# Attention kernel on one core: the last transpose of each turn group reads plain float32, and the mask matmul moves one place forward

## The chip, the core and the metric

The kernel runs on one core of a Trainium2 chip. The metric is the device time of one launch in microseconds (us); the median of three runs is compared. The core has a matrix engine (PE, with its weight loads shown apart as PEld), a vector engine (DVE), an activation engine (ACT), a general engine (POOL), and a queue engine (SP) that issues most of the transfers. Each engine works through its own list in order and waits for semaphores that the others raise.

## The reference

For 4 sequences of 1024 tokens of width 256, with 16 heads of head width 128 plus 64 rotary columns:

```
xn     = layernorm(x)
kv_c   = xn @ W_kvd + b_kvd;   q_c = xn @ W_qd + b_qd            # 64 and 192 wide
keys   = [heads(kv_c @ W_ku + b_ku), rope(heads(kv_c @ W_kr + b_kr))]
query  = [heads(q_c @ W_qu + b_qu),  rope(heads(q_c @ W_qr + b_qr))]
scores = query . keys / sqrt(192), causal
ctx    = softmax(scores) @ heads(kv_c @ W_vu + b_vu)
out    = x + ctx @ W_o + b_o + xn @ binarized(W_ffn).T + b_ffn
```

## The kernel before, in words

The weight products are folded once at the start, so that a head's keys and values are the 64-wide latent itself. Precision is kept by splitting operands into a high and a low part, each in the 4-byte single-pass format (float32r), and adding the products.

The heads go in pairs: 8 pairs for each of 4 sequences, so 32 pair steps. A pair step has 4 blocks, g, numbered n = 0 to 3 inside the pair. A block takes one long and one short row tile of 128 queries, (7,0), (6,1), (5,2), (4,3), for both heads, which makes 4 score items (g, x) with x from 0 to 3, and 9 tiles of 128 keys for each head. The scores of an item go into one of two PSUM slots, `ring[0]` and `ring[1]`, which items and the projections of the next pair use in turn. DVE takes them out with their row minimum (`minimum`, L1086, semaphore `min_ready`); ACT makes the exponentials (L788, `exp_ready`), which lie in `probs` as float32; `probs_r` is the same memory under the single-pass type.

The exponentials must be transposed before they are multiplied with the values. That is done in 5 turn groups for each block, 640 in all: 4 of them have 2 key tiles, so 4 transposes of 128x128, and one has a single tile, so 2 transposes. `turn_group` writes a group into one of two PSUM banks `turn` and raises `turn_full` with its last transpose. ACT copies the bank to `probs_hi` (L797), DVE subtracts to make `probs_lo` (L1096) and raises `turned_ready`, after which the bank is free for the group after the next, and `weigh_group` (L1585, L1586) may multiply. ACT then takes the product out (`u_hi`, L802), PE multiplies with the output weights (`output`, L1609, L1610) and DVE accumulates (L1133).

The causal mask is a bfloat16 matmul of an identity with a mask tile (`mask`, L1522): it opens the accumulation in the score slot of a later item, and the score matmuls (L1539 to L1541) add to it. It is issued inside a turn group, ahead of that group's last transpose. Before it, PE waits until the slot has been left (`slot_left`): by `minimum` of the item two entries earlier, or by ACT's copy (L702) of a projection (L1509). There are 512 masks.

All orders, on PE as on ACT and DVE, are written out by hand: each engine has a `sequence(g)` with the steps of the four blocks. On PE a pair step is, in short: projection of the next pair's rotary keys, output, two turn groups, weighing, scores, and so on, with 20 turn groups, 15 of which carry masks. In three of the 8 pair steps of a sequence, the first three sequences also do the next sequence's work: float32 transposes of its normalized input (`begin("transpose")`, L1437, written with the same call as the turn groups but with plain float32 operands), its down projections (L1448), its feed-forward product (L1454) and its natural-order latent (L1464).

Of the kernel before, what the change touches and what calls it, by code (L numbers as in the profile page):

```python
# [34 lines left out]
P = 128  # L35
# [62 lines left out]
def is_block(g):  # L98
    return 0 <= g < STEPS * BLOCKS
# [36 lines left out]
def build(nc, x, W_kvd, b_kvd, W_ku, b_ku, W_vu, b_vu, W_kr, b_kr, W_qd, b_qd, W_qu, b_qu, W_qr, b_qr,  # L136
# [21 lines left out]
    with ExitStack() as ctx:  # L158
        def sb(name, shape, dt=F32):
            return ctx.enter_context(nc.sbuf_tensor(name, shape, dt))  # L160
# [4 lines left out]
        ident_r, ident_bf, mask_bf = sb("ident", [P, P], F32R), sb("ident_bf", [P, P], BF16), sb("mask_bf", [P, P], BF16)  # L165
        ident = ident_r[:, :].bitcast(F32)
# [65 lines left out]
        turn = [ctx.enter_context(nc.psum_tensor(f"turn{i}", [P, 512], F32)) for i in range(2)]  # L232
        turn_r = [bank[:, :].bitcast(F32R) for bank in turn]
# [61 lines left out]
        def slot_of(entry):  # L295

            return ITEM[entry] % 2
# [9 lines left out]
        def groups_of(g):  # L307

            return [(w, qt, kt, min(2, qt + 1 - kt)) for w, qt in enumerate(LONG_SHORT[g % BLOCKS])
                    for kt in range(0, qt + 1, 2)]  # L310

        def probs_of(g, w, h):

            long, short = LONG_SHORT[g % BLOCKS]
            return probs[g % 2][h][:, (long + 1) * P * w:][:, 0:((long, short)[w] + 1) * P]

        def probs_turned(g, w, h, kt):

            long, short = LONG_SHORT[g % BLOCKS]
            return probs_r[g % 2][h][:, ((long + 1) * w + kt) * P:][:, 0:P]  # L320
# [1080 lines left out]
        def _(pe):  # L1401
            def slot_left(entry):


                if ITEM[entry] < 2:
                    return
                what, owner, k = ENTRIES[ITEM[entry] - 2]
                if what == "score":
                    pe.wait_ge(min_ready, owner * SCORE_ITEMS + k + 1)
                elif what == "project":  # L1410
                    pe.wait_ge(evacuated, owner * PROJ_ITEMS + k + 1)
                elif what == "transpose":
                    pe.wait_ge(xnt_ready, owner * 2 + k + 1)
                elif what == "down":
                    pe.wait_ge(down_ready, owner * 2 + k + 1)
                elif what == "linear":
                    pe.wait_ge(linear_ready, owner * 2 + k + 1)
                elif what == "bias":
                    pe.wait_ge(bias_left, 1)
                else:  # L1420
                    pe.wait_ge(nat_left, owner * 2 + k + 1)
# [94 lines left out]
            def mask(g, x):  # L1516

                if not is_block(g):
                    return
                qt, entry = LONG_SHORT[g % BLOCKS][x % 2], ("score", g, x)  # L1520
                slot_left(entry)
                pe.matmul(ring[slot_of(entry)][:, KEY_COLUMN[qt] + qt * P:KEY_COLUMN[qt] + (qt + 1) * P], ident_bf[:, :], mask_bf[:, :],  # L1522
                          start=True, stop=False, skip_group_check=True)
# [21 lines left out]
            def turn_group(g, i, *masked):  # L1545

                if not is_block(g):
                    for block_g, x in masked:
                        mask(block_g, x)
                    return  # L1550
                w, qt, first_kt, tiles = groups_of(g)[i]
                r = g * GROUPS + i
                if first_kt == 0:
                    pe.wait_ge(exp_ready, g * SCORE_ITEMS + 3 + w)
                if r >= 2:

                    pe.wait_ge(turned_ready, r - 1)
                for t in range(tiles):
                    for h in range(2):
                        kt = first_kt + t  # L1560
                        if (t, h) == (tiles - 1, 1):
                            for block_g, x in masked:
                                mask(block_g, x)
                        mm = pe.transpose(turn_r[r % 2][:, (2 * t + h) * P:(2 * t + h + 1) * P],  # L1564
                                          probs_turned(g, w, h, kt), ident_r[:, :])
                mm.then_inc(turn_full, 1)

            def weigh_group(g, i):
# [56 lines left out]
            def sequence(g):  # L1625
# [3 lines left out]
                if n == 0:  # L1629
                    project(g, ROPE_K)  # L1630
                    output(g - 3, 1)
                    turn_group(g - 1, 0)
                    turn_group(g - 1, 1, (g, 0))
                    weigh_group(g - 2, 3)
                    weigh_group(g - 2, 4)
                    head_ready(g, 0)
                    scores(g, 0, 0)
                    scores(g, 0, 1)
                    turn_group(g - 1, 2, (g, 1))
                    output(g - 2, 0)  # L1640
                    weigh_group(g - 1, 0)
# [244 lines left out]
```

## Time and profile before

| | |
|---|---|
| median of 3 runs | 1408.62 us (1408.5 to 1410.0) |
| the profiled execution's own time | 1410.69 us |
| its span in the profile | 1408.9 us |
| mean granted clock of TensorE | 0.997 of full speed |
| busy: PE, PEld, DVE, ACT, POOL | 97%, 87%, 81%, 85%, 71% |

The span is the time from the first to the last instruction of the profiled execution. PE's busy time is the union of its matmul records; one record lasts from its start to a modelled end, and records of neighbours overlap. The distance from one start to the next is therefore more telling than the length of a record.

### The profile page before, as it was taken

How to read it: one execution, taken by the hardware profiler on the slowest of the kernel's cores; microseconds unless marked ns; L12 is line 12 of the kernel's file. 1: busy time of each engine (PE TensorE's matmuls, PEld its weight loads, DVE VectorE, ACT ScalarE, POOL GpSimd, SP SyncE). 2: the span in 40 equal slices, each digit the busy share in tenths (PEclk: the TensorE clock that was granted, in tenths of full speed). 3: DMA queues.
4: the chain of work that ended last, by engine and by line, in shares of the span. 5: the costliest groups of instructions: out<-in, count | busy, mean ns of one | idle time of the engine just before them, and what ended most of it. 6: DMA issues, size and time to landing. Idle time of an engine off the chain costs nothing.

```text
span 1408.9 us, 27603 instructions
## 1 busy us (share of the span) xinstructions
PE 1373.1 (97%) x9786; PEld 1229.7 (87%) x9786; DVE 1146.4 (81%) x2708; ACT 1200.5 (85%) x2603; POOL 1000.4 (71%) x573
## 2 busy tenths in 40 slices
PE   6979999999999999999999999999999999999998
PEld 4769999997898999888899999999789999999987
DVE  4858898885788888887688889888678888888898
ACT  4659889997788988998788999899878988889887
POOL 6986777777667777769666787777766877777750
PEclk9999999999999999999999999999999999999999
DMA  9851222212343322211333222222233322221110
GB/s 274 228 127 50 72 54 64 64 50 64 76 107 79 83 64 64 64 34 47 79 94 92 64 80 64 65 57 57 63 77 87 88 64 65 64 60 45 40 31 31
DMA packets 46957, 106.82 MB, mean 76 GB/s; under 512 B 9333, under 2 KB 17830, under 8 KB 46822
## 3 DMA queue, kind: packets, MB, share of 16 engines
q1 hardware_dynamic: 43360, 94.01, 26.0%
q0 software_dynamic: 3296, 11.01, 2.8%
q8 instruction: 80, 1.31, 0.4%
q14 instruction: 55, 0.45, 0.1%
q10 hardware_dynamic: 166, 0.03, 0.0%
HBM read 48.92 MB, written 9.96 MB: 42 GB/s over the span
## 4 chain that ended last, share of the span: by engine, by line
PE 79%; ACT 7%; POOL 5%; DVE 5%; DMA 2%; issue 1%; SPq 1%; POOLq 0%; ACTq 0%; DVEq 0%
PE ring L1509 11%; PE turn L1564 10%; PE u_ps L1585 9%; PE ring L1539 9%; PE ring L1540 8%; PE ring L1541 8%; PE u_ps L1586 8%; PE o_ps L1609 4%; PE o_ps L1610 4%; PE ring L1522 3%; ACT probs L788 2%; PE ring L1448 2%; PE ring L1454 2%; DVE probs L1086 1%; DVE probs_lo L1096 1%; POOL k_rope L377 1%
## 5 line engine op out<-in xcount | busy, mean ns | idle before, releaser
L1086 DVE TENSOR_SCALAR_CACHE_REDUCE probs<-ring,c_t 128x1024 f32<-128x1024 f32 (+7 forms) x512 | 413.2, 809 | 85.7 <-PE ring L1541 85.2
L1096 DVE TENSOR_TENSOR probs_lo<-turn,probs_hi 128x512 fp32r<-128x512 f32 (+1 forms) x640 | 401.0, 630 | 65.7 <-ACT probs_hi L797 61.0
L797 ACT ACTIVATE probs_hi<-turn 128x512 fp32r<-128x512 f32 (+1 forms) x640 | 346.4, 550 | 94.0 <-PE turn L1564 91.2
L788 ACT ACTIVATE probs<-probs,row_min 128x1024 f32<-128x1024 f32 (+7 forms) x512 | 394.5, 772 | 11.8 <-DVE probs L1086 9.5
L1564 PE MATMUL turn<-ident,probs_r 128*128 128x128 f32 x2304 | 315.9, 244 | 4.6 <-DVE probs_lo L1096 2.7
L1585 PE MATMUL u_ps<-probs_hi,kv_nat 128*128 128x256 f32 x1147 | 313.5, 301 | 1.2 <-DVE u_pair L1102 1.2
L1564 PEld LDWEIGHTS turn<-ident,probs_r 128*128 128x128 f32 x2304 | 267.9, 141 | 36.5 <-DVE probs_lo L1096 15.3
L1586 PE MATMUL u_ps<-probs_lo,kv_nat 128*128 128x256 f32 x1147 | 289.7, 281 | 0.0
L1539 PE MATMUL ring<-k_hi,q_hi 128*128 128x512 f32 (+3 forms) x768 | 273.6, 356 | 0.0
L1540 PE MATMUL ring<-k_lo,q_hi 128*128 128x512 f32 (+3 forms) x768 | 262.9, 342 | 0.0
L1541 PE MATMUL ring<-k_hi,q_lo 128*128 128x512 f32 (+3 forms) x768 | 262.7, 342 | 0.0
L1133 DVE SCALAR_TENSOR_TENSOR acc<-o_ps,row_inv,acc 128x256 f32<-128x256 f32 x474 | 227.0, 479 | 31.6 <-PE o_ps L1610 28.2
L1585 PEld LDWEIGHTS u_ps<-probs_hi,kv_nat 128*128 128x128 f32 x1147 | 216.2, 189 | 5.4 <-DVE u_pair L1102 1.8
L1586 PEld LDWEIGHTS u_ps<-probs_lo,kv_nat 128*128 128x128 f32 x1147 | 217.1, 189 | 0.0
L388 POOL TENSOR_TENSOR k_lo<-k_rope,k_hi 64x1024 fp32r<-64x1024 f32 x62 | 148.5, 2396 | 48.7 <-ACT k_hi L766 46.3
L377 POOL TENSOR_TENSOR q_x<-q_x,cos 64x1024 f32<-64x1024 f32 x31 | 74.5, 2404 | 129.3 <-DMA swapped<-q_x 129.3
L377 POOL TENSOR_TENSOR k_rope<-k_rope,cos 128x1024 f32<-128x1024 f32 x31 | 74.6, 2407 | 128.2 <-DMA swapped<-k_rope 127.9
L1541 PEld LDWEIGHTS ring<-k_hi,q_lo 128*128 128x128 f32 x768 | 144.9, 189 | 14.0
L377 POOL TENSOR_TENSOR swapped<-swapped,sin 128x1024 f32<-128x1024 f32 x62 | 149.0, 2403 | 4.9
L1540 PEld LDWEIGHTS ring<-k_lo,q_hi 128*128 128x128 f32 x768 | 145.1, 189 | 6.9
L1539 PEld LDWEIGHTS ring<-k_hi,q_hi 128*128 128x128 f32 x768 | 144.4, 188 | 7.4
L1609 PE MATMUL o_ps<-wv,u_hi 128*128 128x256 f32 x506 | 140.3, 299 | 1.5 <-DVE acc L1133 1.5
(229 smaller groups left out, 2585.8 us busy)
## 6 DMA issues: line engine op xcount, KB each, us to landing
swapped<-k_rope SPq DMA_DIRECT2D x128, 128.0 KB, 2.3
wv<-wv_scratch SPq DMA_DIRECT2D x62, 256.0 KB, 4.0
wp<-wp_scratch SPq DMA_DIRECT2D x62, 192.0 KB, 3.5
wp<-wp_scratch SPq DMA_DIRECT2D x31, 256.0 KB, 3.1
swapped<-q_y SPq DMA_DIRECT2D x62, 128.0 KB, 2.3
swapped<-q_x SPq DMA_DIRECT2D x62, 128.0 KB, 2.3
k_hi<-qb_kv_hi SPq DMA_DIRECT2D x16, 256.0 KB, 3.7
k_lo<-qb_kv_lo SPq DMA_DIRECT2D x16, 256.0 KB, 5.0
```

The source lines that it names most:

```text
L377: engine.tensor_tensor(to, a, b, op).then_inc(rope_step, 1)
L788: act.activation(p, p, ACT.Exp, scale=-1.0, bias=row_min[:, r:r + 1], accum_out=row_sum[:, g % 4, w, h:h + 1]).then_inc(exp_ready, 1)
L797: act.activation(probs_hi[:, r % 4, 0:width], turn[r % 2][:, 0:width], ACT.Identity).then_inc(turned_hi, 1)
L1086: dve.tensor_scalar(probs_of(g, w, h), ring[slot_of(entry)][:, KEY_COLUMN[qt]:KEY_COLUMN[qt] + keys], c_t[b % 2][:, qt, ds(pair * 2 + h, 1 ...
L1096: dve.tensor_tensor(probs_lo[:, r % 4, 0:width], turn[r % 2][:, 0:width], probs_hi[:, r % 4, 0:width].bitcast(F32), ALU.subtract).then_inc ...
L1133: dve.scalar_tensor_tensor(out=acc[:, qt, :], in0=o_bank(g, w)[:, h, :], scalar=inv, in1=start[:, qt, :], op0=ALU.mult, op1=ALU.add).then_ ...
L1539: pe.matmul(to, qh, kh[:, keys], start=not masked, stop=False, skip_group_check=masked)
L1540: pe.matmul(to, qh, kl[:, keys], start=False, stop=False, skip_group_check=masked)
L1541: mm = pe.matmul(to, ql, kh[:, keys], start=False, stop=True, skip_group_check=masked)
L1564: mm = pe.transpose(turn_r[r % 2][:, (2 * t + h) * P:(2 * t + h + 1) * P], probs_turned(g, w, h, kt), ident_r[:, :])
L1585: pe.matmul(u_bank(g, w), kv_nat[:, kt, :], probs_hi[:, r % 4, cols], start=(kt == 0), stop=False)
L1586: mm = pe.matmul(u_bank(g, w), kv_nat[:, kt, :], probs_lo[:, r % 4, cols], start=False, stop=(kt == qt))
```

## The change

In `turn_group` the last transpose of each group no longer reads the exponentials under the single-pass type with the single-pass identity into the bank's single-pass view. It reads the same memory as plain float32, with the same identity as plain float32, into the plain float32 view of the same bank. The other transposes stay. The masks are issued ahead of the third of 4 transposes in place of the fourth; in a group of 2 they stay ahead of the second.

```diff
-                for t in range(tiles):
-                    for h in range(2):
-                        kt = first_kt + t
-                        if (t, h) == (tiles - 1, 1):
-                            for block_g, x in masked:
-                                mask(block_g, x)
-                        mm = pe.transpose(turn_r[r % 2][:, (2 * t + h) * P:(2 * t + h + 1) * P],
-                                          probs_turned(g, w, h, kt), ident_r[:, :])
+                turns = [(t, h) for t in range(tiles) for h in range(2)]
+                for n, (t, h) in enumerate(turns):
+                    if n == max(len(turns) - 2, 1):
+                        for block_g, x in masked:
+                            mask(block_g, x)
+                    kt, columns = first_kt + t, slice((2 * t + h) * P, (2 * t + h + 1) * P)
+                    if n < len(turns) - 1:
+                        pe.transpose(turn_r[r % 2][:, columns], probs_turned(g, w, h, kt), ident_r[:, :])
+                    else:
+                        mm = pe.transpose(turn[r % 2][:, columns], probs_of(g, w, h)[:, kt * P:(kt + 1) * P], ident)
                 mm.then_inc(turn_full, 1)
```

## Rows read from the trace of the kernel before

**Rows 1.** The page: busy time by engine, and the chain's shares by engine.
```profile
PE 1373.1 (97%) x9786; PEld 1229.7 (87%) x9786; DVE 1146.4 (81%) x2708; ACT 1200.5 (85%) x2603; POOL 1000.4 (71%) x573
...
PE 79%; ACT 7%; POOL 5%; DVE 5%; DMA 2%; issue 1%; SPq 1%; POOLq 0%; ACTq 0%; DVEq 0%
```

**Rows 2.** Waits of ACT: who waited for whom, us, times, longest.
```profile
ACT probs_hi L797 <- PE turn L1564: 91.2, 76, 3.1
```

**Rows 3.** The mask's line L1522: what its idle time ended with (us, times).
```profile
  ACT q_x L702: 3.8, 23
```

**Rows 4.** Timeline of weight loads, both transpose kinds: start us, us, what, count.
```profile
983.70 0.14 PEld L1564 LDWEIGHTS turn<-ident,probs_r 128*128 128x128 f32 x1
983.78 0.14 PEld L1437 LDWEIGHTS ring<-ident,xn 128*128 128x128 f32 x1
...
983.84 0.25 PEld L1437 LDWEIGHTS ring<-ident,xn 128*128 128x128 f32 x2
...
984.50 0.14 PEld L1437 LDWEIGHTS ring<-ident,xn 128*128 128x128 f32 x1
984.61 0.19 PEld L1585 LDWEIGHTS u_ps<-probs_hi,kv_nat 128*128 128x128 f32 x1
984.72 0.19 PEld L1586 LDWEIGHTS u_ps<-probs_lo,kv_nat 128*128 128x128 f32 x1
```

**Rows 5.** Timeline of matmuls: a single-pass last transpose, and eight plain ones.
```profile
794.80 0.26 PE L1564 MATMUL turn<-ident,probs_r 128*128 128x128 f32 x1
...
983.82 1.06 PE L1437 MATMUL ring<-ident,xn 128*128 128x128 f32 x8
```

**Rows 6.** Timeline of weight loads around three masks of one pair, and the next.
```profile
794.39 0.32 PEld L1564 LDWEIGHTS turn<-ident,probs_r 128*128 128x128 f32 x3
794.76 0.10 PEld L1522 LDWEIGHTS ring<-mask_bf,ident_bf 128*128 128x128 bf16 x1
794.78 0.14 PEld L1564 LDWEIGHTS turn<-ident,probs_r 128*128 128x128 f32 x1
794.86 0.19 PEld L1539 LDWEIGHTS ring<-k_hi,q_hi 128*128 128x128 f32 x1
794.97 0.19 PEld L1540 LDWEIGHTS ring<-k_lo,q_hi 128*128 128x128 f32 x1
...
801.38 0.10 PEld L1522 LDWEIGHTS ring<-mask_bf,ident_bf 128*128 128x128 bf16 x1 [0.16 <-ACT q_x L702]
...
814.35 0.10 PEld L1522 LDWEIGHTS ring<-mask_bf,ident_bf 128*128 128x128 bf16 x1
...
833.94 0.10 PEld L1522 LDWEIGHTS ring<-mask_bf,ident_bf 128*128 128x128 bf16 x1
```

**Rows 7.** Timeline of ACT in the same pair.
```profile
795.10 0.60 ACT L797 ACTIVATE probs_hi<-turn 128x512 fp32r<-128x512 f32 x1 [2.03 <-PE turn L1564]
...
797.16 0.39 ACT L802 ACTIVATE u_hi<-u_ps 128x256 fp32r<-128x256 f32 x1
...
800.21 1.12 ACT L702 ACTIVATE q_x<-ring,bias_p 128x1024 f32<-128x1024 f32 x1
...
816.47 0.38 ACT L797 ACTIVATE probs_hi<-turn 128x256 fp32r<-128x256 f32 x1 [0.27 <-PE turn L1564]
```

**Rows 8.** Timeline of DVE in the same pair.
```profile
810.71 0.48 DVE L1086 TENSOR_SCALAR_CACHE_REDUCE probs<-ring,c_t 128x256 f32<-128x256 f32 x1 [0.25 <-PE ring L1541]
...
813.29 1.00 DVE L1086 TENSOR_SCALAR_CACHE_REDUCE probs<-ring,c_t 128x768 f32<-128x768 f32 x1
...
832.61 1.27 DVE L1086 TENSOR_SCALAR_CACHE_REDUCE probs<-ring,c_t 128x1024 f32<-128x1024 f32 x1
```

**Rows 9.** Busy time of each engine in two stretches.
```profile
816.47:831.97 15.50, 15.49 (x119) 14.15 (x119) 13.74 (x34) 15.30 (x35) 13.66 (x6) 1.00 0.22 69
...
321.33:343.96 22.63, 22.63 (x126) 17.27 (x125) 12.03 (x29) 18.10 (x31) 13.55 (x8) 1.00 0.20 53
```

## The prediction

> **What bounds the kernel now.** I read the page first. PE is busy 97% of the span, ACT 85%, DVE 81%, and the chain of waits puts 79% on PE [rows 1]. That looks like a kernel that gains whatever PE gains. It is not the whole truth: a PE record has a modelled end and overlaps its neighbours, so a wait of 0.1 us inside a run of short matmuls is still counted as busy. So I went on to the waits, and then followed one ordinary pair step (39.2 us) in the timelines of PEld, ACT and DVE.
>
> ACT is the engine to look at. It waits for a transposed bank 76 times, 91.2 us in all [rows 2], two or three times in each of the 32 pair steps, and between these waits it runs without a pause: from 816.47 to 831.97 us it is busy for 15.30 of 15.50 us [rows 9]. Three masks of a pair step are late because of such runs. Together they form a loop that closes after 39.18 us, from the mask at 794.76 to the one at 833.94 [rows 6]:
>
> - Stretch A. The mask goes at 794.76; the last transpose of its group follows; ACT has been idle 2.03 us for it and starts at 795.10 [rows 7]. ACT then works through to the copy of a projection, `q_x`, 800.21 to 801.33, and the mask at 801.38 waited for exactly that [rows 6, 7]. This wait is idle time on PEld in 23 pairs [rows 3]. PE does nothing that sets the time between 795.1 and 801.4, but for a product that ACT takes out at 797.16, where both sides arrive nearly together.
> - Stretch B. From 801.38 PE runs through scores and projections until a score item is full, at which DVE, idle 0.25 us, starts at 810.71; DVE works its list to the minimum that begins at 813.29 and lasts 1.00, and the mask goes at 814.35 [rows 6, 8].
> - Stretch C. The mask at 814.35, its transpose, a few matmuls and a group of two transposes, for which ACT has been idle 0.27 us; ACT starts at 816.47 [rows 7], runs to about 832, and the DVE minimum that begins at 832.61 and lasts 1.27 releases the mask at 833.94 [rows 6, 8].
>
> So of 39.2 us, PE sets the time in some 0.3 + 9.3 + 2.1 us; the rest is set by ACT and DVE, with PE just in time. What PE saves elsewhere becomes a longer wait.
>
> **The change part by part.** The trace has plain float32 transposes to compare with: 8 in a row behind a turn group (L1437). I read PE's pace from the distances between weight loads: they go one for one with the matmuls, and no modelled end blurs them.
>
> *Entry.* From the load of a single-pass transpose to the next load 0.08 to 0.09 us pass (983.70 to 983.78; 794.78 to 794.86, there with the mask ahead of it; three loads that end after 0.32 with 0.14 each make (0.32 - 0.14)/2 = 0.09). From a plain load that follows a single-pass transpose to the next load it is 0.06 (983.78 to 983.84) [rows 4, 6]. So a plain transpose gets in 0.03 us sooner. I apply the same 0.03 where the mask is directly ahead (groups of two); the trace has no such pair of neighbours, so the bounds are 0 and 0.03.
>
> *Exit.* A plain transpose streams 0.11 us: two loads in 0.25 us, 0.14 each [rows 4]. That is about twice a single-pass one. But the matmul behind it needs 0.11 us for its own weights in either case: 794.86 to 794.97 behind a single-pass one, 984.61 to 984.72 behind plain ones [rows 4, 6]. Behind a single-pass transpose this load lies bare, behind a plain one it is hidden. So the longer streaming costs nothing on PE; the cover is the next load, and where another transpose follows instead (1 group in 20) it costs 0.11 - 0.09 = 0.02.
>
> On PE alone that is 640 x 0.03, less 32 x 0.02: about 18.6 us saved. I don't credit it outside the stretches above.
>
> *Later end.* The bank is full later. The single-pass record ends at 794.80 + 0.26 = 795.06, 0.20 after the next load begins (794.86); eight plain ones end at 983.82 + 1.06 = 984.88, 0.27 after 984.61 [rows 4 to 6]. ACT gets the bank 0.07 later, less the 0.03 of the entry: +0.04. It is hidden wherever ACT has other work, which is most places, but not at the two starts of stretches A and C.
>
> *The mask, one place forward.* Where the mask doesn't wait, nothing but order changes. At the three late masks it matters. Before, the third transpose was done while PE waited: its load begins about 0.18 after 794.39, the mask goes 0.19 later at 794.76 [rows 6]. After the change it stands behind the mask. From the mask to the matmul behind the group is then 0.09 + 0.06 + 0.11 = 0.26 us in place of 0.09 + 0.11 = 0.20: +0.06 at each late mask. What queues behind it is the group's own end, and ACT waits for that.
>
> *Sum of one loop.* A: the bank is full 0.06 + 0.07 = 0.13 later if ACT's list sets the time, or PE's product is 0.06 - 0.03 = 0.03 later if that does; the two are level at 797.16, so I take the middle, +0.08 (bounds 0.03 and 0.13). B: +0.06 at the mask, less three groups on PE's way at 0.03: -0.03. C: +0.06 at the mask, +0.04 for the group of two whose end ACT waits for: +0.10. Sum +0.15 us a pair, bounds 0.10 and 0.20.
>
> 23 pairs have the loop for certain [rows 3]: +3.5 us. The other nine carry the next sequence's work or stand at the ends. Three of them have a stretch of 22.63 us in which PE is busy throughout and ACT for 18.10 [rows 9]: there six groups give back 0.18 against one late mask at 0.06. The others have one or two of the three late masks. I put the nine at +0.5 together, between -0.4 and +1.4. Total +4.0 us.
>
> The largest unknown is the entry. The 0.03 comes from transposes that change PSUM bank at that point; the new ones don't. If inside one bank a plain transpose takes 0.09 like its neighbours, each term loses its 0.03: A +0.12, B +0.09, C +0.09 + 0.07, together +0.37, over 23 to 32 pairs +8.5 to +11.8.
>
> A page's rule speaks against the change far more strongly. The Trainium skill, "FP8 and Floating Point Precision", section "TensorE Precision Notes", says that true FP32 takes four passes through the array. This trace doesn't agree for transposes: 0.11 against 0.06 is two, not four [rows 4].
>
> **Rivals.**
>
> 1. *Slower by the loop, as summed:* +2.3 to +6. Median 1412.6.
> 2. *PE's order sets the end after all, faster.* For it: 97% and 79% [rows 1]. Against it: ACT's 15.30 of 15.50 [rows 9] and the named wait at the masks [rows 3]. Its price: 18.6 us saved less 3 x 23 late masks that lose 0.06 and don't gain 0.03, 6.2 us: about -12, so 1396. It decides as soon as ACT and DVE reach the late masks some 0.1 us earlier than now, or if only half the saving comes through, 1402.
> 3. *No difference.* The later bank at 795.10 might be absorbed by the level meeting at 797.16, and the ends of the groups by ACT's list: the loop then keeps only B and half of C, about +0.03 a pair, +1 us: 1409.6.
> 4. *The plain entry costs 0.09 in the same bank:* 1417 to 1420.
> 5. *Four passes.* A plain transpose would stream 4 x 0.06 = 0.24, of which 0.11 is hidden; 640 x (0.24 - 0.11 - 0.03) = 64 us, about 1473. The trace's eight plain transposes speak against it [rows 4]. This is the rule of the page named above.
>
> **How the numbers follow.** The profiled execution took 1410.69 us for a span of 1408.9, 1.8 us around it; the median of the runs is 1408.62, so the sum of +4.0 is added to the median: 1412.6. Chances: rival 1 0.58, rival 2 0.16, rival 3 0.15, rival 4 0.09, rival 5 0.02. The runs can tell about 0.2%, 2.8 us, from no change. Of rival 1, the part below +2.8 is a quarter: 0.14 same and 0.44 slower. Rivals 4 and 5 are slower, rival 3 same; of rival 2 0.14 is faster and 0.02 same. So faster 0.14, same 0.31, slower 0.55. The range holds rivals 1, 3 and most of 4 and the weak end of 2: 1405 to 1419. Most of the chance is on no gain; the likeliest case alone is 1410.9 to 1414.6.
>
> **What the changed profile would show.** The load behind the group's plain transpose follows 0.06 after the plain load began (0.09 would be rival 4), and the one behind that 0.11 later. The three late masks stay late, with more idle time ahead of them: the mask's wait for `q_x` grows from 3.8 us, by some 0.2 a time. ACT's wait for the bank behind the first late mask grows from 2.03. The pair step grows from 39.18 to some 39.33. If instead the mask's waits shrink, or the pair step falls under 39.1, rival 2 is right and this forecast wrong; it would also be wrong if plain and single-pass transposes as neighbours cost something that no row here shows.

## The result, and the profile after

The changed kernel is slower: 1414.79 us median of 5 runs against 1408.62, a ratio of 1.0036 with a 95% interval of 1.0024 to 1.0047, which is +5.1 us (+3.4 to +6.6); the two medians alone lie 6.2 apart. The profiled span went from 1408.9 to 1412.9 us at the same granted clock of 0.997. The forecast was 1412.6.

The page of the changed kernel, busy time by engine and the chain's shares by engine, beside [rows 1]:

```profile
PE 1370.0 (97%) x9786; PEld 1217.8 (86%) x9786; DVE 1148.9 (81%) x2708; ACT 1200.5 (85%) x2603; POOL 1000.1 (71%) x573
...
PE 63%; ACT 25%; DVE 4%; POOL 3%; DMA 2%; issue 1%; SPq 1%; POOLq 0%; ACTq 0%; DVEq 0%
```

PE and PEld are busy for less time than before (1370.0 against 1373.1 us, 1217.8 against 1229.7), and the kernel takes longer: what PE gained became waiting. The chain now puts 25% on ACT, where it had 7%.

ACT's waits, beside [rows 2] (total us, times, longest):

```profile
ACT probs_hi L797 <- PE turn L1567: 99.8, 102, 3.1
```

L1565 is the single-pass transpose in the changed kernel, L1567 the plain last one. The 26 additional entries are for the most part not new waits: the view lists a wait only when it is longer than 0.15 us. Call the late mask that opens the prediction's stretch A mask A, and so for B and C. 23 of the 26 are ACT's wait for the group at mask C (block 1, group 2), which grew from 0.05 to 0.21 us (medians). In the kernel before, that copy is the second of this row, and no wait is listed with it:

```profile
814.05 1.23 ACT L797 ACTIVATE probs_hi<-turn 128x512 fp32r<-128x512 f32 x2
```

What the mask's idle time ended with (us, times), beside [rows 3]:

```profile
  ACT q_x L702: 7.9, 27
  DVE probs L1086: 3.1, 13
```

These counts have the same limit. In the kernel before, four more pairs wait 0.14 to 0.15 us for `q_x` at this mask and are not listed, so it is 27 pairs in both kernels. What did grow is the wait itself. The idle time of PE's weight loads ahead of the three late masks went from 0.06 to 0.15 us at A, from 0.16 to 0.30 at B and from 0.02 to 0.14 at C (medians over the 32 pair steps).

Now the weight loads of one pair step, the same one as in [rows 6]: the first late mask with its neighbours, then the two other late masks and the next pair's first.

```profile
795.75 0.22 PEld L1565 LDWEIGHTS turn<-ident,probs_r 128*128 128x128 f32 x2
796.12 0.10 PEld L1522 LDWEIGHTS ring<-mask_bf,ident_bf 128*128 128x128 bf16 x1
796.14 0.14 PEld L1565 LDWEIGHTS turn<-ident,probs_r 128*128 128x128 f32 x1
796.23 0.14 PEld L1567 LDWEIGHTS turn<-ident,probs 128*128 128x128 f32 x1
796.26 0.22 PEld L1539 LDWEIGHTS ring<-k_hi,q_hi 128*128 128x128 f32 x1
796.40 0.19 PEld L1540 LDWEIGHTS ring<-k_lo,q_hi 128*128 128x128 f32 x1
...
802.80 0.10 PEld L1522 LDWEIGHTS ring<-mask_bf,ident_bf 128*128 128x128 bf16 x1 [0.30 <-ACT q_x L702]
...
815.82 0.10 PEld L1522 LDWEIGHTS ring<-mask_bf,ident_bf 128*128 128x128 bf16 x1
...
835.53 0.10 PEld L1522 LDWEIGHTS ring<-mask_bf,ident_bf 128*128 128x128 bf16 x1
```

Between the second transpose and the mask PE loads nothing (two loads from 795.75, over at 795.97, then none until 796.12). Before, the third transpose ran in that gap; now it and the plain one both stand behind the mask. From the mask's load to the first score load behind the group it is 0.14 us (796.12 to 796.26) in place of 0.10, and to the second 0.28 in place of 0.21. From mask A to the next mask A the step is 39.41 us (796.12 to 835.53), where it was 39.18.

The engine that waits for this bank is ACT (timeline, beside [rows 7]):

```profile
796.60 0.60 ACT L797 ACTIVATE probs_hi<-turn 128x512 fp32r<-128x512 f32 x1 [2.12 <-PE turn L1567]
...
798.61 0.37 ACT L802 ACTIVATE u_hi<-u_ps 128x256 fp32r<-128x256 f32 x1
...
801.63 1.12 ACT L702 ACTIVATE q_x<-ring,bias_p 128x1024 f32<-128x1024 f32 x1
...
816.30 0.60 ACT L797 ACTIVATE probs_hi<-turn 128x512 fp32r<-128x512 f32 x1 [0.21 <-PE turn L1567]
...
818.06 0.39 ACT L797 ACTIVATE probs_hi<-turn 128x256 fp32r<-128x256 f32 x1 [0.26 <-PE turn L1567]
```

From mask A to ACT's start it is 0.48 us now (796.12 to 796.60), 0.34 before: +0.14. From there to `q_x` it is 5.03 in place of 5.11, so 0.08 of it is absorbed on the way, 0.05 of that up to `u_hi` (2.01 in place of 2.06). The wait at 816.30, for the group at mask C, is now long enough to be listed, and from mask C to the copy of the group of two it is 2.24 us (815.82 to 818.06) in place of 2.12.

DVE's two steps of stretch B, beside [rows 8]:

```profile
812.17 0.48 DVE L1086 TENSOR_SCALAR_CACHE_REDUCE probs<-ring,c_t 128x256 f32<-128x256 f32 x1 [0.27 <-PE ring L1541]
...
814.76 1.00 DVE L1086 TENSOR_SCALAR_CACHE_REDUCE probs<-ring,c_t 128x768 f32<-128x768 f32 x1
```

From mask B to DVE's start it is 9.37 us (9.33 before), from there to mask C 3.65 (3.64): DVE's part didn't change.

### The profile page after: what moved, and what is told of

It reads as the page before. It is cut to its first block, busy times and chain, and to the rows that moved or that the text cites. A ratio compares the mean times of both kernels' runs of the same rounds, so it can differ in the third digit from the quotient of the medians.

```text
span 1412.9 us, 27603 instructions
## 1 busy us (share of the span) xinstructions
PE 1370.0 (97%) x9786; PEld 1217.8 (86%) x9786; DVE 1148.9 (81%) x2708; ACT 1200.5 (85%) x2603; POOL 1000.1 (71%) x573
## 4 chain that ended last, share of the span: by engine, by line
PE 63%; ACT 25%; DVE 4%; POOL 3%; DMA 2%; issue 1%; SPq 1%; POOLq 0%; ACTq 0%; DVEq 0%
ACT probs L788 10%; PE u_ps L1587 7%; PE ring L1541 6%; PE ring L1540 6%; PE ring L1539 6%; PE ring L1509 6%; PE u_ps L1588 6%; PE turn L1565 6%; ACT probs_hi L797 5%; PE turn L1567 4%; PE o_ps L1611 3%; PE o_ps L1612 3%; ACT u_pair L811 3%; PE ring L1522 3%; PE ring L1448 2%; ACT q_x L702 2%
## 5 line engine op out<-in xcount | busy, mean ns | idle before, releaser
L1587 PE MATMUL u_ps<-probs_hi,kv_nat 128*128 128x256 f32 x1147 | 316.8, 304 | 1.3 <-DVE u_pair L1102 1.3
L1565 PE MATMUL turn<-ident,probs_r 128*128 128x128 f32 x1664 | 261.4, 243 | 6.0 <-DVE probs_lo L1096 2.5
L1565 PEld LDWEIGHTS turn<-ident,probs_r 128*128 128x128 f32 x1664 | 209.3, 141 | 40.3 <-DVE probs_lo L1096 16.1
L1587 PEld LDWEIGHTS u_ps<-probs_hi,kv_nat 128*128 128x128 f32 x1147 | 222.3, 194 | 6.1 <-DVE u_pair L1102 1.9
L1567 PE MATMUL turn<-ident,probs 128*128 128x128 f32 x640 | 187.8, 293 | 0.0
L1539 PEld LDWEIGHTS ring<-k_hi,q_hi 128*128 128x128 f32 x768 | 150.0, 195 | 7.3
```

Of the source, the lines that this page charges most:

```text
L1539: pe.matmul(to, qh, kh[:, keys], start=not masked, stop=False, skip_group_check=masked)
L1565: pe.transpose(turn_r[r % 2][:, columns], probs_turned(g, w, h, kt), ident_r[:, :])
L1567: mm = pe.transpose(turn[r % 2][:, columns], probs_of(g, w, h)[:, kt * P:(kt + 1) * P], ident)
L1587: pe.matmul(u_bank(g, w), kv_nat[:, kt, :], probs_hi[:, r % 4, cols], start=(kt == 0), stop=False)
```

## How the runs are compared

The four medians of the kernel before lie between 1408.6 and 1410.6 us, its single runs between 1407.0 and 1413.6, so I also read two things from each trace, which scatter less. An ordinary pair step is one without the next sequence's work.

- **Pair step:** the distance between successive copies of `k_rope` on ACT (L702, or the same copy under its shifted line; one per pair step), as the median of 14 ordinary steps, the same 14 in every trace.
- **A, B, C:** the distances between the loads of the three late masks, medians over 13 ordinary pair steps, the same 13 in every trace.

| kernel | median us (its own before) | ratio, 95% | pair step | A | B | C |
|---|---|---|---|---|---|---|
| before | 1408.62 | | 39.23 | 6.609 | 13.016 | 19.608 |
| after | 1414.79 (1408.62) | 1.0036 [1.0024, 1.0047] | 39.43 | 6.677 | 13.031 | 19.716 |
| e1 plain, masks in old place | 1409.74 (1410.26) | 0.9994 [0.9985, 1.0003] | 39.19 | 6.600 | 12.940 | 19.645 |
| e2 masks forward, single-pass | 1414.97 (1410.26) | 1.0032 [1.0020, 1.0045] | 39.50 | 6.700 | 13.084 | 19.704 |
| e3 after, late masks in old place | 1409.66 (1410.26) | 0.9994 [0.9985, 1.0004] | 39.17 | 6.594 | 12.950 | 19.626 |
| e4 before, late masks behind group | 1408.20 (1410.26) | 0.9984 [0.9975, 0.9992] | 39.06 | 6.577 | 12.971 | 19.511 |
| e5 more PE work in C | 1411.95 (1410.17) | 1.0010 [1.0001, 1.0020] | 39.25 | 6.613 | 13.021 | 19.617 |
| e6 more PE work in B | 1415.34 (1410.17) | 1.0035 [1.0023, 1.0047] | 39.41 | 6.612 | 13.184 | 19.617 |
| e7 more ACT work in C | 1416.49 (1410.17) | 1.0049 [1.0036, 1.0062] | 39.51 | 6.611 | 13.002 | 19.899 |
| e8 late masks behind, 15 groups plain | 1404.86 (1410.17) | 0.9957 [0.9944, 0.9970] | 39.00 | 6.566 | 12.892 | 19.539 |
| e9 after, one group of B single-pass | 1415.96 (1410.55) | 1.0038 [1.0025, 1.0050] | 39.44 | 6.683 | 13.029 | 19.720 |
| e10 after, one group of C single-pass | 1413.57 (1410.55) | 1.0023 [1.0014, 1.0032] | 39.39 | 6.682 | 13.027 | 19.680 |
| e11 late masks behind, all plain | 1406.97 (1410.55) | 0.9971 [0.9962, 0.9980] | 39.06 | 6.556 | 12.884 | 19.613 |

## The experiments

The theory is the prediction's: three late masks form a loop through PE, ACT and DVE, and only work on this loop sets the time. The main rival is that PE's order sets the end, as its 97% says.

### The two parts of the change, one at a time

e1, on the changed kernel: the format alone.

```diff
-                    if n == max(len(turns) - 2, 1):
+                    if n == len(turns) - 1:
```

> Plain last transposes as in the changed kernel, masks back in their old place (ahead of the last transpose). Loop theory (three late masks and the bank's later end set the time): from a late mask to the matmul behind the group it is now 0.02 us shorter than before, the bank is full 0.04 to 0.05 later; over a pair step -0.05 us (bounds -0.10 and +0.03), so the span is 1407.3, between 1405.5 and 1409.5, and the pair step 39.15 to 39.25. Rival, format theory (mixing the two formats costs the time itself, in every group): as the changed kernel, span 1412 to 1414. Rival, PE's order sets the end: 640 x 0.025 = 16 us saved, span near 1393.

e2, on the kernel before: the masks alone.

```diff
-                        if (t, h) == (tiles - 1, 1):
+                        if 2 * t + h == max(2 * tiles - 2, 1):
```

> All transposes in the single-pass format, only the masks one place forward. Loop theory: at each of the three late masks one more transpose of 0.085 us stands behind the wait, +0.25 us a pair step over 23 to 28 pairs: span 1415 to 1416, pair step 39.45 to 39.50, more than the changed kernel, which gets part of it back by the quicker entry. Format theory: no difference from before, 1408.9. PE's order sets the end: the late masks' three transposes alone, +6 to +7, so this run does not tell it from the loop theory.

The format alone makes no difference that can be measured (0.9994), and the masks alone make all of the loss (1.0032). By stretches, the masks alone cost 0.09, 0.07 and 0.10 us in A, B and C: in each case about one single-pass transpose, the third one, which now stands behind the mask (0.08 to 0.09 from one load to the next, [rows 4]). The format alone gives 0.01 in A and 0.08 in B, where PE runs through, and costs 0.04 in C. Together that is +0.26 and -0.05, sum +0.21; the whole change has 0.07 + 0.015 + 0.11, so +0.19. The two parts add up to within 0.02.

e1 is also the clearest run against the rival. The plain transposes are there in all 640 groups and PE has less to do (about 0.02 us in each, see the entry below), and the time stays. And the mask's waits grow without any loss (e1, what the mask's idle time ended with):

```profile
  ACT q_x L702: 5.8, 27
```

That is 5.8 us in place of 3.8, at the same 27 pairs, and the pair step is 0.04 shorter. So the wait of 7.9 in the changed kernel is not the price of the change either: part of it is only PE arriving earlier.

### Which masks

e3, on the changed kernel: only the masks of the three late items go back, 3 of 16 in a pair step.

```diff
+                    late = any((block_g % BLOCKS, x) in ((0, 2), (1, 0), (2, 2)) for block_g, x in masked)
-                    if n == max(len(turns) - 2, 1):
+                    if n == (len(turns) - 1 if late else max(len(turns) - 2, 1)):
```

> The changed kernel, with the masks of only three places (items 2 of block 0, 0 of block 1 and 2 of block 2) put back ahead of the last transpose; the other eight of the moved ones stay forward. Loop theory: those three carry the whole loss, so the span is that of the run with all masks back, within 1 us: 1406 to 1410. Format theory: 1412 to 1414, as the changed kernel. If the other masks matter too (newly late ones), it lies in between, above 1410.

The whole loss is gone (pair step 39.17, as with all masks in the old place, 39.19). Nine other masks of a pair step stay one place forward in e3 and cost nothing; the last four are in groups of two and were never moved.

e4, on the kernel before: the same three masks go the other way, behind their group's last transpose.

```diff
+                late = any((block_g % BLOCKS, x) in ((0, 2), (1, 0), (2, 2)) for block_g, x in masked)
-                        if (t, h) == (tiles - 1, 1):
+                        if (t, h) == (tiles - 1, 1) and not late:
...
                 mm.then_inc(turn_full, 1)
+                if late:
+                    for block_g, x in masked:
+                        mask(block_g, x)
```

> The kernel before, with the three late masks put behind their group's last transpose. Loop theory: the bank no longer waits for the mask, and behind the mask only the next weight load (about 0.12 us) stands in place of a transpose and that load (0.20): -0.08 us at each, ACT's start 0.2 earlier, so -0.24 us a pair step: span 1401 to 1403. If ACT's lists leave no slack at their far ends, less: 1405. Format theory and PE's order have no reason for more than 0.08 x 3 x 23 = 5.5 us either, but under PE's order the gain would come without ACT's wait of 2.03 us getting shorter.

The sign turns: 0.9984, pair step 39.06. In e4's loads around mask A, the group of four is complete before the mask, and ACT starts 0.20 after the mask's load (timeline of weight loads, then of ACT):

```profile
790.81 0.40 PEld L1565 LDWEIGHTS turn<-ident,probs_r 128*128 128x128 f32 x4
791.19 0.10 PEld L1522 LDWEIGHTS ring<-mask_bf,ident_bf 128*128 128x128 bf16 x1
791.26 0.19 PEld L1539 LDWEIGHTS ring<-k_hi,q_hi 128*128 128x128 f32 x1
```

```profile
791.39 0.60 ACT L797 ACTIVATE probs_hi<-turn 128x512 fp32r<-128x512 f32 x1 [1.90 <-PE turn L1565]
```

So the three positions of the three masks give 39.43 (or 39.50 with single-pass transposes), 39.23 and 39.06 us. The gain of e4, 0.17 a pair, is smaller than the 0.24 that I expected, and it falls on all three stretches (0.03, 0.045 and 0.10). ACT's wait for the bank falls from 2.03 to 1.90 us, as the loop theory asked. In A, ACT starts 0.14 sooner after the mask, and only 0.03 of it is left at `q_x`: ACT now waits 0.05 us for PE's product at `u_hi` (medians), the place where the prediction had both sides level. In the runs the gain is smaller still: 0.17 over 23 pairs would be 3.9 us, and the ratio says 2.3 (1.1 to 3.5). That difference I can't explain.

### What sets the time in which stretch

e5 and e6, both on the kernel before: the first transpose of two groups is issued twice, in C (e5) or in B (e6). The extra transposes write the same values again.

```diff
+                        for again in range(2 if (t, h) == (0, 0) and (g % BLOCKS, i) in ((1, 4), (2, 1)) else 1):
-                        mm = pe.transpose(turn_r[r % 2][:, (2 * t + h) * P:(2 * t + h + 1) * P],
-                                          probs_turned(g, w, h, kt), ident_r[:, :])
+                            mm = pe.transpose(turn_r[r % 2][:, (2 * t + h) * P:(2 * t + h + 1) * P],
+                                              probs_turned(g, w, h, kt), ident_r[:, :])
```

In e6 the pairs are ((0, 2), (0, 3)).

> The kernel before, with the first transpose of two turn groups (block 1, group 4 and block 2, group 1) issued twice; both lie in stretch C, where by the loop theory ACT sets the time. That is two more single-pass transposes of 0.085 us, +0.17 us of PE work in each of 32 pair steps. Loop theory: the pair step stays at 39.2 us (39.17 to 39.27) and the median within 1 us of before, but for the three long pair steps in which PE is busy throughout, which may grow by 0.17 each. Rival, PE's order sets the end: +0.17 a pair, 39.37, and +5.4 us in all.

> The same two extra transposes, but in block 0, groups 2 and 3, which lie in stretch B, where by the loop theory PE runs without waiting from the late mask behind q_x to the score item that DVE waits for. Loop theory: +0.17 us a pair, pair step 39.34 to 39.40, +3.9 us over 23 pairs and up to +5.4 over all 32. If stretch B had slack against DVE: less than +2. The rival, PE's order sets the end everywhere, gives +5.4 here and in the run with the extra transposes in stretch C alike, so the two runs together tell the theories apart.

The same work on PE costs 0.02 us a pair step in C and 0.18 in B. e5's timelines, the five loads of one lengthened group and then two successive copies of `k_rope` on ACT:

```profile
816.69 0.57 PEld L1565 LDWEIGHTS turn<-ident,probs_r 128*128 128x128 f32 x5
```

```profile
789.37 1.11 ACT L702 ACTIVATE k_rope<-ring,bias_p 128x1024 f32<-128x1024 f32 x1
...
828.55 1.11 ACT L702 ACTIVATE k_rope<-ring,bias_p 128x1024 f32<-128x1024 f32 x1
```

The fifth transpose is there, and this step is 39.18 (39.18 in the kernel before, too). The same two rows of ACT in e6 are 39.41 apart:

```profile
789.95 1.11 ACT L702 ACTIVATE k_rope<-ring,bias_p 128x1024 f32<-128x1024 f32 x1
...
829.36 1.11 ACT L702 ACTIVATE k_rope<-ring,bias_p 128x1024 f32<-128x1024 f32 x1
```

In e6 the whole 0.17 lands in B (13.016 to 13.184), A and C stay. The median of e5 is 1.4 us above its before (0.1 to 2.8), a little more than I expected; 0.02 a step makes 0.6 of it, and I haven't placed the rest.

e7, on the kernel before: one copy of ACT in stretch C is made in four pieces.

```diff
+                if (g % BLOCKS, w) == (1, 0):
+                    for c in range(0, 192, 64):
+                        act.activation(u_pair[w][64:P, c:c + 64], u_hi[w][0:64, c:c + 64].bitcast(F32), ACT.Identity)
+                    act.activation(u_pair[w][64:P, 192:], u_hi[w][0:64, 192:].bitcast(F32), ACT.Identity).then_inc(u_copied, 1)
+                else:
+                    act.activation(u_pair[w][64:P, :], u_hi[w][0:64, :].bitcast(F32), ACT.Identity).then_inc(u_copied, 1)
```

> The kernel before, with ACT's copy of one product half (L811, 64x256, 0.42 us) in block 1 made in four pieces of 64 columns. It does the same work with three more instructions of ACT, an estimate of 0.3 to 0.7 us more in stretch C of each pair step, from the 0.27 us that the trace shows for 128x128 and the 0.16 us for one column. Loop theory: the pair step grows by nearly that, 39.5 to 39.9, and the median by +7 to +16 us. Rival, PE's order sets the end and ACT has slack: no change, within 1 us.

ACT's timeline in e7, the four pieces and what follows:

```profile
825.34 0.55 ACT L813 ACTIVATE u_pair<-u_hi 64x64 fp32r<-64x64 f32 x3
825.80 0.24 ACT L814 ACTIVATE u_pair<-u_hi 64x64 fp32r<-64x64 f32 x1
826.06 1.06 ACT L770 ACTIVATE q_hi<-q_x 128x1024 fp32r<-128x1024 f32 x1
```

And the same place in the kernel before:

```profile
820.81 0.41 ACT L811 ACTIVATE u_pair<-u_hi 64x256 fp32r<-64x256 f32 x1
821.25 1.06 ACT L770 ACTIVATE q_hi<-q_x 128x1024 fp32r<-128x1024 f32 x1
```

The pieces take 0.72 us up to the next operation, the one copy 0.44: 0.28 more. The pair step grew by 0.28 (39.51), one for one and all of it in C (19.61 to 19.90), and the median by 6.9 us (5.1 to 8.7). ACT is busy 85% of the span, and yet 0.28 us of its work in stretch C is 0.28 us of time.

### The later end of a bank

Besides the groups with late masks, two groups of the changed kernel hand their bank to an ACT that is already waiting: block 1, group 1 (at the end of B; ACT's wait is only about 0.01 us) and block 1, group 3 (the group of two in C). e9 and e10 are the changed kernel with that one group single-pass again (e10 with (1, 3)):

```diff
+                    elif (g % BLOCKS, i) == (1, 1):
+                        mm = pe.transpose(turn_r[r % 2][:, columns], probs_turned(g, w, h, kt), ident_r[:, :])
                     else:
                         mm = pe.transpose(turn[r % 2][:, columns], probs_of(g, w, h)[:, kt * P:(kt + 1) * P], ident)
```

> The changed kernel, with the last transpose of one group (block 1, group 1) single-pass again; ACT waits for this group's bank at the end of stretch B in the changed trace. Pair step of the changed kernel 39.43. Theory, the plain transpose's later bank end is what turned B's term from -0.03 to +0.05: pair step 39.34 to 39.38, and 1 to 2 us less in the median. Rival, B lost it at its late mask and not at the bank: 39.42 to 39.45, the median of the changed kernel unchanged.

> The changed kernel, with the last transpose of block 1, group 3 single-pass again: the group of two behind the late mask of stretch C, for which ACT has been idle. By the prediction's step for the later bank (+0.04 there): pair step 39.37 to 39.41, 1 us less in the median. If the later end of the bank costs nothing there: 39.43.

My theory for the first fell: 39.44, B as in the changed kernel. The second came as expected: 39.39, C shorter by 0.04.

### A version that beats both

e8 takes e4 and adds the plain last transpose where nobody waits for the bank, 15 of 20 groups; e11 adds it in all 20.

```diff
-                        mm = pe.transpose(turn_r[r % 2][:, (2 * t + h) * P:(2 * t + h + 1) * P],
-                                          probs_turned(g, w, h, kt), ident_r[:, :])
+                        if (t, h) == (tiles - 1, 1) and not late and (g % BLOCKS, i) not in ((1, 1), (1, 3)):
+                            mm = pe.transpose(turn[r % 2][:, (2 * t + h) * P:(2 * t + h + 1) * P],
+                                              probs_of(g, w, h)[:, kt * P:(kt + 1) * P], ident)
+                        else:
+                            mm = pe.transpose(turn_r[r % 2][:, (2 * t + h) * P:(2 * t + h + 1) * P],
+                                              probs_turned(g, w, h, kt), ident_r[:, :])
```

> The kernel with the three late masks behind their group's last transpose, and in addition the plain float32 last transpose in every group but the three with late masks and two whose bank ACT waits for (block 1, groups 1 and 3): 15 of 20 groups. Loop theory: three of these groups lie on PE's way in stretch B and save 0.02 each, so the pair step is 38.97 to 39.06 (39.04 to 39.08 with the masks moved alone), the long PE-bound pair steps lose 0.2 to 0.3, and the median is 1 to 3 us under that of the masks moved alone, 3 to 5.5 under the kernel before. If the format is worth nothing anywhere: level with the masks moved alone, some 2.2 under the kernel before.

> The kernel with the three late masks behind their group's last transpose, with plain float32 last transposes in all 20 groups of a pair step (15 in the run that was the fastest, pair step 39.00). Theory, the later bank end costs where ACT waits for the bank (three late groups and two more): pair step 39.05 to 39.15, and 1 to 4 us above the fastest run. Rival, the later end is nowhere on the path: 38.95 to 39.00.

e8 has the shortest pair step, 39.00, and a ratio of 0.9957: 6 us faster than the kernel before. The format, worth nothing where PE waits, gives 0.08 us in B against e4, as in e1 against the kernel before. With all groups plain the step is 39.06: C is 0.07 longer than in e8, while A and B are 0.01 shorter each, so it is the later bank that costs there: from mask C to the copy of the group of two it is 2.14 us in e11 and 2.05 in e8 (medians). Between e4 and e8 the ordinary steps explain 0.06 us times some 28 steps, 1.7 us; the ratios lie about 3.8 us apart. The traces can't show the rest: the profiled execution was the fastest of e4's eleven runs and the second slowest of e8's six.

The page of e8 (busy time, and the chain by engine):

```profile
PE 1366.0 (97%) x9786; PEld 1222.2 (87%) x9786; DVE 1145.0 (82%) x2708; ACT 1203.4 (86%) x2603; POOL 1000.7 (71%) x573
...
PE 72%; ACT 14%; DVE 5%; POOL 3%; DMA 3%; SPq 2%; issue 1%; POOLq 0%; DVEq 0%; ACTq 0%
```

Nothing in these lines says that this kernel is some 10 us faster than the changed one.

## Why the prediction was right, step by step

**The mechanism** was right, and it was shown: the loss sits at three masks of a pair step (e3), it changes sign with their position (e4), PE work counts in B and not in C (e5, e6), ACT work counts in C in full (e7). That ACT and PE share stretch A, and DVE's part in B and C, are read from the timelines and from e4; no run added work there.

**The loop's sum** was +0.15 a pair (0.10 to 0.20), and it is +0.20, at the edge.

- A: +0.08 forecast, +0.07 measured. The bank came 0.14 later for ACT (0.13 in the working), and about half of it was absorbed on the way to `q_x`.
- B: -0.03 forecast, +0.015 measured. This is the term that was mis-sized. After the late mask PE is 0.07 behind (0.06 in the working), and each of the three groups on PE's way gives back 0.02 and not 0.03: the second load behind the late mask's group stands at +0.07 against the kernel before, the second loads behind the three groups at +0.04, +0.02 and +0.01 (medians over the 13 pair steps). The last 0.01 falls among the matmuls behind the third group and has no cause that I could show; e9 excludes the bank that I suspected.
- C: +0.10 forecast, +0.11 measured; the group of two has 0.04 of it, as forecast (e10).

**The entry** of the plain transpose was the largest unknown, and it was sized 0.03. The loads don't stand as I read them from the neighbours before: the load behind a plain transpose follows after 0.04 us, not 0.06, and the one behind that after 0.13 to 0.14, not 0.11 (796.23, 796.26, 796.40). Up to the second load it is 0.17, just what the working had. A single-pass transpose takes 0.19 over the same two (0.085 and 0.108 in median) where the working had 0.20, so a group gains 0.02. The working's largest unknown was that its row changes PSUM bank and the new transposes don't: inside one bank the sum is 0.17 as well, also where the mask stands directly ahead (e1, 0.06 and 0.12). Rival 4 needed 0.09 for the first distance and is out.

**The total** was +4.0: 23 pairs with +3.5, the others +0.5. By the pair step it is 23 x 0.20 = 4.6, and the ratio says 5.1 (3.4 to 6.6). That the spans lie just 4.0 apart is luck. From copy to copy of `k_rope`, 23 of the 31 steps grew, by 0.14 to 0.46 and by 4.9 us together, and seven others by 0.1 together; one fell by 1.02, because in the trace before it took 41.30, and between 40.16 and 40.86 in the twelve other traces. The 23 pairs of the working were counted by waits that the view lists, those over 0.15 us; 27 pairs have the wait. The median of the runs, 1414.79, lies within the range and just above the likeliest case's own range, which ended at 1414.6. The give-back in the three long pair steps, -0.12 each, didn't show: from copy to copy of `k_rope` they are 53.8 us before and after.

**The rivals.** PE's order as the limit (rival 2, 1396) is excluded by e1 and e5. Note what spoke for it: PE 97% and a chain with 79% on PE. The Trainium skill, "Perfetto Trace Analysis", section "Identifying the Most-Contended Engine", says not to judge TensorE by its matmul busy share but by its MFU, the part of the peak arithmetic that the kernel does, and by the share of its weight loads. This case agrees on the matmul share (97%, and e5's additional matmuls cost 0.02 us a step) and shows the limit of the weight loads' share: PEld's busy time fell by 11.9 us, from 87% to 86%, while the kernel got slower. No difference (rival 3) would have needed +0.03 a pair. Four passes (rival 5) would have put the second load behind a plain transpose 0.24 or more behind it; it stands 0.17 behind.

**What the changed profile was to show.** The late masks stayed late, ACT's 2.03 grew to 2.12, the pair step grew. The wait for `q_x` grew from 0.17 to 0.29 us a time (listed waits, 3.8 over 23 and 7.9 over 27), less than the 0.2 more that I named, and e1 shows that this was a poor sign in any case: there it grows with no loss.

## What to carry to other kernels

Where two engines keep each other just in time, look for the few instructions that release a wait in both directions, here three masks in a pair step of some 300 matmuls; put ahead of them everything that doesn't need them, and behind them what does. A cheaper instruction pays only on the stretches in which its engine runs through, so find these first: adding a known 0.17 us to one stretch at a time shows it more surely than the busy shares. And a saving can shorten the work and still lengthen the time, if its result arrives later for the engine that is waiting.

## What the hardware showed that I had not expected

- How soon the next weight load begins behind a plain float32 transpose depends on what stood ahead of that transpose. With a transpose directly ahead and a matmul behind, it is 0.037 us, and 0.134 more to the load after (medians over 401 groups of the changed kernel). With the mask directly ahead, as in e1, it is 0.057 and 0.117 (380 groups). The sum is 0.17 both times, and only the sum is a price; read alone, the first distance looks like a gain of 0.05. The lines of e1, beside those at 796.23 to 796.40 of the changed kernel:

```profile
794.52 0.14 PEld L1567 LDWEIGHTS turn<-ident,probs 128*128 128x128 f32 x1
794.58 0.19 PEld L1539 LDWEIGHTS ring<-k_hi,q_hi 128*128 128x128 f32 x1
794.69 0.19 PEld L1540 LDWEIGHTS ring<-k_lo,q_hi 128*128 128x128 f32 x1
```

- The chain of waits moves from 79% to 63% PE, and to 72% in the fastest kernel, for differences of 0.1 us at a few places; in e1, which takes the same time as the kernel before, it stands at 60%. Where two engines arrive together, its shares say little about what a change would bring.
